# Flamingo block on one core: a new order of a layer unit, paired normalisations, resident inputs and two weight slots, with the bias accumulator in SBUF

## The reference

```python
for i in range(L):                                   # L = 4
    y = _attention(_norm(x), ctx, dist, mask, Wq[i], Wk[i], ...)   # 16 heads of 64
    x = x + y
    y = relu(_norm(x) @ Wf1[i] + bf1[i]) @ Wf2[i] + bf2[i]         # 512 wide
    x = x + y
# in _attention:
hbias   = relu(dist[..., None] @ Wth + bth)          # K = 32 terms for each pair of tokens
qs_bias = (hbias @ Wto + bto)[..., 0]
logits  = q k / 8 + mask + qs_bias                   # the same bias for all heads
```

## Time and profile before

| what | value |
|---|---|
| median of 3 runs | 1356.88 us (1356.79 to 1357.87) |
| profiled execution, its own time | 1357.18 us |
| span from the first to the last instruction | 1355.5 us |
| mean granted TensorE clock | 0.985 |
| first score, last F score group | 58.18 us, 1343.3 us |

### The profile page before, as it was taken

The page is one execution under the profiler, slowest core; times in us unless marked ns, Lnnn a source line. Parts: engine busy times, 40 slices in busy tenths (PEclk is TensorE's granted clock), DMA queues, the critical chain, the costliest instruction groups (busy, mean ns, idle before and its releaser), DMA issues.

```text
span 1355.5 us, 37243 instructions
## 1 busy us (share of the span) xinstructions
PE 1240.9 (92%) x11184; PEld 1020.6 (75%) x11184; DVE 1227.6 (91%) x4922; ACT 1061.2 (78%) x3353; POOL 854.1 (63%) x889
## 2 busy tenths in 40 slices
PE   1599999999999999999999999999999999799998
PEld 1377878787878787878787878788777878677776
DVE  4899999999999999999999999999999988488886
ACT  4588878887888888888888888788887866388886
POOL 3677777777777777777777777777777743111110
PEclk9799999999999999999999999999999999799999
DMA  5201010102110100022000000111101000000000
GB/s 148 75 5 30 14 32 14 32 13 79 46 33 13 29 17 24 22 70 55 24 22 24 22 20 24 59 47 29 31 13 44 13 14 11 5 21 21 23 16 9
DMA packets 69190, 42.21 MB, mean 31 GB/s; under 512 B 14840, under 2 KB 63872, under 8 KB 68992
## 3 DMA queue, kind: packets, MB, share of 16 engines
q1 hardware_dynamic: 68992, 39.84, 10.2%
HBM read 23.29 MB, written 1.05 MB: 18 GB/s over the span
## 4 chain that ended last, share of the span: by engine, by line
DVE 27%; PE 24%; ACT 22%; issue 20%; POOL 5%; DMA 1%; DVEq 1%; ACTq 0%; SPq 0%; POOLq 0%
ACT prob L802 13%; DVE bias_acc L951 7%; ACT relu_z L785 5%; PE L L688 4%; POOL sd L1391 4%; PE M L582 4%; PE O L552 4%; DVE score L998 3%; DVE hid L1073 3%; DVE qT L1123 3%; PE T L695 2%; DVE st L1016 2%; PE M L762 2%; DVE rs L1025 2%; ACT probT L809 1%
## 5 line engine op out<-in xcount | busy, mean ns | idle before, releaser
L802 ACT ACTIVATE prob<-score,nmax 128x128 f32<-128x128 f32 x1024 | 396.8, 391 | 156.5 <-DVE nmax L998 156.4
L1396 POOL TENSOR_TENSOR prob<-prob,rinv 128x512 f32<-128x512 f32 x256 | 291.6, 1139 | 178.4 <-DVE rinv L1006 173.2
L951 DVE SCALAR_TENSOR_TENSOR bias_acc<-relu_z,cst,bias_acc 128x512 f32<-128x512 f32 x370 | 349.8, 945 | 3.5 <-ACT relu_z L785 0.2
L785 ACT ACTIVATE relu_z<-dist_g,cst 128x512 f32<-128x512 f32 x386 | 295.1, 804 | 16.8 <-DMA cst<-cst_all 16.8
L998 DVE CUSTOM_DVE_ANT_0 score<-L,bias 128x128 f32<-128x128 f32 x1024 | 234.0, 281 | 2.7 <-PE L L528 1.6
L1391 POOL TENSOR_TENSOR sd<-mv,half 128x1 f32<-128x1 f32 x128 | 127.7, 998 | 118.3 <-DVE mv L1018 117.1
L802 ACT ACTIVATION_READ_ACCUMULATOR prob<-score,nmax 128x1 f32 x1024 | 193.6, 189 | 0.0
L538 PE MATMUL T<-ident,prob 128*128 128x128 f32 x1024 | 161.3, 280 | 4.8 <-POOL prob L1396 2.5
L582 PE MATMUL M<-wv,ctxT 128*128 128x512 f32 x256 | 145.6, 651 | 17.9 <-DVE hid L1073 13.0
L552 PEld LDWEIGHTS O<-probT,v 128*64 128x64 f32 x2048 | 109.7, 136 | 59.7 <-issue 51.9
L528 PE MATMUL L<-kT,qT 64*128 64x128 f32 x2048 | 149.7, 286 | 0.0
(11 more groups left out here) (134 smaller groups left out, 2225.8 us busy)
## 6 DMA issues: line engine op xcount, KB each, us to landing
dist_g<-in_fside_BxSxS SPq DMA_DIRECT2D x16, 256.0 KB, 2.9
mask_g<-in_mask_Bx1x1xS_ff SPq DMA_DIRECT2D x16, 256.0 KB, 3.5
ctxT<-ctxT_all SPq DMA_DIRECT2D x64, 64.0 KB, 1.9
xs<-x_all SPq DMA_DIRECT2D x64, 64.0 KB, 1.8
x_all<-xs SPq DMA_DIRECT2D x64, 64.0 KB, 1.8
wk<-in_L_xattn_Wk SPq DMA_DIRECT2D x4, 512.0 KB, 4.3
wv<-in_L_xattn_Wv SPq DMA_DIRECT2D x4, 512.0 KB, 5.4
wq<-in_L_xattn_Wq SPq DMA_DIRECT2D x4, 512.0 KB, 5.5
```

Source lines behind the costliest of these rows:

```text
L785: nc.scalar.activation(relu_z[:, z_slot(g, k), :], dist_g[:, :, :], ACT.Relu, bias=cst[:, C_BTH + k:C_BTH + k + 1], scale=cst[:, C_WTH + k ...
L802: last = nc.scalar.activation(prob[:, c, m, :], score[:, c, m, :], ACT.Exp, bias=nmax[:, c, m:m + 1], scale=-1.0, accum_out=rsum[:, c, m:m ...
L951: vec.scalar_tensor_tensor(out=bias_acc[:, :], in0=relu_z[:, z_slot(g, k), :], scalar=weight, in1=bias_acc[:, :], op0=ALU.mult, op1=ALU.ad ...
L1396: gp.tensor_tensor(prob[:, c, :, :], prob[:, c, :, :], rinv[:, c, :].rearrange("p (m o) -> p m o", o=1).broadcast_to([P, 4, P]), ALU.mult) ...
```

## The change

The units keep their work, and each engine has a new list. Bias terms: DVE takes 22 of a group and POOL 10; the accumulator `bias_acc` stays in SBUF. dist, mask, constants, x and context stay resident and are read in place, so the small copies by DMA go; the weights have two slots. The two normalisations of a step (the second of unit i-1 and the first of unit i+1) are done together: one root of two columns, one copy of both turned halves. `hid` is one instruction of 128x512; the hidden bias is folded into it and into the bias of the output. ACT makes all four copies of turned probabilities and both of the queries, DVE both of the keys and half of the output copies. The eight PSUM banks are shared out anew: the second score bank is the feed-forward bank (B0). In the F block the two groups of scores are written in turn, row group against row group.

```diff
-VEC_K = 24
-POOL_K = BIAS_K - VEC_K
+VEC_K = 22
+POOL_K = BIAS_K - VEC_K
+Z_PLAN = ((1, 1, 1, 3), (1, 1, 1, 3), (1, 1, 1, 2), (1, 1, 1, 2))
+TERM_PLAN = ((1, 1, 3, 1), (1, 1, 3, 1), (1, 1, 2, 1), (1, 1, 2, 1))
+POOL_PLAN = ((1, 2, 5), (1, 2, 5), (1, 2, 4), (1, 2, 4))
...
-cst = sb("cst", [P, C_ALL])
+dist_all = sb("dist_all", [P, BATCHES, P])
+mask_all = sb("mask_all", [P, BATCHES, P])
+wq = sb("wq", [P, 2, HEADS * HD])
+ACC = sb("bias_acc", [P, GROUP * P])
+hh = sb("hh", [P, 2, 2, P])
...
+S_BANK = [B[2], B[0], B[6], B[1]]
+T_BANK = [B[5], B[2], B[1], B[3]]
+K_BANK, V_BANK, Q_BANK, O_BANK = [B[2], B[3]], [B[4], B[1]], [B[6], B[4]], [B[4], B[5]]
+WO_BANK, HH_BANK, FF_BANK = B[3], B[6], B[0]
...
+    def scores(u, octet):
+        s = u % 2
+        if octet == 0:
+            pe.wait_ge(k_kept, upto(u, 2, 1))
+            pe.wait_ge(q_kept, upto(u, 2, 1))
+            wait(pe, pT_kept, upto(u - 1, 4, 1))
+            wait(pe, hid_kept, upto(u - 2))
...
-    def f_scores(g, i, c):
-        wait(pe, fexp, after(g, i, 4, c - 2))
-        rows = slice(32 * c, 32 * c + 32)
-        for j in range(ROW_HEADS):
-            last = mm(L[c % 2][:, j * P:(j + 1) * P], qm[rows, i % 2, j, :], kF[rows, i % 2, :], start=True, stop=True)
-        last.then_inc(fqk, 1)
+    def f_scores(g, i, half_):
...
+        wait(pe, fexp, after(g, i, 4, 2 * half_ - 1))
+        for j in range(ROW_HEADS):
+            for a in range(2):
+                c = 2 * half_ + a
+                rows = slice(32 * c, 32 * c + 32)
+                last = mm(L[a][:, j * P:(j + 1) * P], qm[rows, i % 2, j, :], kF[rows, i % 2, :], start=True, stop=True)
...
+    def inverse_deviation(i):
+        s, h = (i + 1) % 2, halves(i)
...
+    def normalise(u, a):
...
+        vec.tensor_scalar(hh[:, s, a, :], x_all[:, b, :], mv[:, s, a, 0:1], rs[:, s, a:a + 1],
+                          ALU.subtract, ALU.mult).then_inc(hb_done if a else ha_done, 1)
+    def keep_pair(i):
+        s, h = (i + 1) % 2, halves(i)
+        dve.wait_ge(hh_done, pairs(i))
...
+        vec.tensor_copy(hhT[:, s, h, :], src).then_inc(hh_kept, 1)
...
-                last = vec.tensor_scalar(hid[:, i % 2, c, :], M1[:, c * P:(c + 1) * P], bf1c[:, c:c + 1], 0.0, ALU.add, ALU.max)
+    def hidden(u):
...
+        vec.tensor_tensor(hid[:, u % 2, :, :], FF_BANK[:, :].rearrange("p (c t) -> p c t", c=CHUNKS),
+                          nb1_all[:, l, :].rearrange("p (c o) -> p c o", o=1).broadcast_to([P, CHUNKS, P]),
+                          ALU.max).then_inc(hid_kept, 1)
...
-        gp.tensor_tensor(sd[:, a, s:s + 1], mv[:, a, s, 1:2], half[:, 0:1], ALU.pow).then_inc(sdev[a], 1)
+    def root(i):
...
+        gp.tensor_tensor(sd[:, s, h], mv[:, s, h, 1], half[:, 0:h.stop - h.start], ALU.pow).then_inc(rooted, 1)
...
+    def step(i):
+        cur, prev = there(i), there(i - 1)
+        plan = POOL_PLAN[i % GROUP]
+        if cur:
+            norm(i, 0)
+            ops(plan[0])
+            norm(i, 1)
...
+            f_root(0, F_EARLY.index(i), 0)
+        if cur:
+            norm(i, 2)
+            ops(plan[1])
+        if prev:
+            plus_bias(i - 1)
+        if cur:
+            norm(i, 3)
```

More of the change, by code:

```diff
@@ L38 @@
 BIG = 3.0e38
-VEC_K = 24
+VEC_K = 22
 POOL_K = BIAS_K - VEC_K
 START_VEC_K = 26
-START_POOL_SKIP = START_VEC_K - VEC_K
-POOL_FIRST = 2
+START_POOL_K = BIAS_K - START_VEC_K
 Z_SLOTS = 6
[L49 to L83, removed]
+Z_LEAD = 3
+POOL_LEAD = 6
+Z_PLAN = ((1, 1, 1, 3), (1, 1, 1, 3), (1, 1, 1, 2), (1, 1, 1, 2))
+TERM_PLAN = ((1, 1, 3, 1), (1, 1, 3, 1), (1, 1, 2, 1), (1, 1, 2, 1))
+POOL_PLAN = ((1, 2, 5), (1, 2, 5), (1, 2, 4), (1, 2, 4))
+assert sum(map(sum, Z_PLAN)) == sum(map(sum, TERM_PLAN)) == VEC_K
+assert sum(map(sum, POOL_PLAN)) == 3 * POOL_K
+START_Z = (6, 4, 4, 3)
+START_STATS = (4, 4, 6)
+F_EARLY = (UNITS - 3, UNITS - 2)
+F_FIRST_PARTS = ((0, 1), (2, 3, 4, 5, 6), (7, 8, 9), (10, 11))
 C_WTH, C_BTH, C_WTO = 0, BIAS_K, 2 * BIAS_K
@@ L270, in block_program @@
         block = stack.enter_context(nc.Block())
[L272 to L294, removed]
@@ L498, in _ @@
+            for i in range(BATCHES):
+                sp.wait_ge(fout, i + 1)
+                sp.dma_start(out[i, :, :], outF[:, i % 2, :]).then_inc(out_st[i % 2], 16)
             for a in range(2):
@@ new lines, in ffn2 @@
+            def ffn2(u):
+                weights(u, w_f2)
+                pe.wait_ge(hid_kept, upto(u))
+                if there(u + 2):
+                    pe.wait_ge(scored, upto(u + 2, 4, 1))
+                for c in range(CHUNKS):
+                    last = mm(FF_BANK[:, 0:P], hid[:, u % 2, c, :], wf2[:, slot_of(u), c, :], start=c == 0, stop=c == CHUNKS - 1)
+                last.then_inc(f2_done, 1)
+            def step(i):
+                nxt, cur, prev, old = there(i + 1), there(i), there(i - 1), there(i - 2)
+                if cur:
+                    scores(i, 0)
+                    scores(i, 1)
@@ L1142, in f_first @@
+                if nxt:
+                    keep_keys(i + 1, 1)
+                more(2)
+                if prev:
+                    hidden(i - 1)
+                more(3)
+                if cur and i % GROUP == GROUP - 1 and i + 1 < UNITS:
+                    finish_bias(i // GROUP + 1)
             def f_first(g, i, part):
@@ L1372, in ahead @@
                     vec.tensor_scalar(bq_mask[:, :], head_mask[:, :], bqk[:, 0:1], None, ALU.mult).then_inc(f_consts, 1)
[L1374 removed]
+            f_step(0, -1)
+            step(UNITS)
+            f_step(0, 0)
+            residual2(UNITS - 1)
+            for i in range(1, BATCHES + 1):
+                f_step(0, i)
         @block.gpsimd
@@ new lines, in _, with ops, plus_bias @@
+            op_next = 0
+            def ops(n):
+                nonlocal op_next
+                for j in range(op_next, min(op_next + n, 3 * len(POOL_TERMS))):
+                    (product, clamp, add)[j % 3](j // 3, *POOL_TERMS[j // 3])
+                op_next += n
+            def plus_bias(u):
+                l = u // BATCHES
+                pool.wait_ge(resid1, upto(u))
+                wait(pool, resid2, upto(u - 2))
+                pool.wait_ge(bf_kept, l + 1)
+                gp.tensor_tensor(xb[:, u % 2, :], x_all[:, u % BATCHES, :], b2f[:, l % 2, :], ALU.add).then_inc(xb_done, 1)
```

1182 lines of the change are left out of this document (545 added, 637 removed).

## The result

The changed kernel takes 1369.78 us, median of four runs (1367.89 to 1371.05); the kernel before took 1356.84 beside it. The ratio is 1.0094 (95% interval 1.0077 to 1.0112): slower by 0.9%, where faster by 0.9% was forecast. The profiled execution takes 1371.05 us, its span is 1369.3 against 1355.5.

The account below looks back on a forecast made before the run. DVE, 95.5% busy, was taken to bound the layers, PE the F block. 1357.2 - 4 (start) + 1.5 (layers) - 9 (F block), less 0.3 for the median, gave 1345 us; range 1270 to 1390.

Parts of the forecast that it names:

- steady layers: Layer units: DVE's loop from `hid` to `hid`, 69.2 us a group against 69.1; +1.5 us over 15 groups.
- The F block: F units: scores in turn on two row groups save 0 to 1.27 us a unit; 0.6 taken, -9 us over 15 units.
- the start: Before the first scores: constants read in place let bias terms start up to 4.6 us earlier; -4 us taken.
- The waits between terms and POOL: Layers: a term waits for POOL's running instruction and ends 0.55 us after it; pairs take 1.68 or 1.18.
- the tosses: Layers: two near-ties between term and POOL, costing 0.63 and 0.76 us if lost; half counted, 68.5 to 69.2 a group.
- The price of `sde`: Layers: two-column `sde` may wait for POOL's second `norm`, up to 0.9 us a unit, +55; left outside the sum.
- the slower rival: Layers: POOL goes ahead at the second `h` in every step, +50 us less 10 already counted, 1385 us; chance 0.17.
- PE does not bind: Layers: PE's 16.4 us busy time a unit is partly waiting matmuls, its weight loads 13.7; PE sets no pace.

Follow-up runs that it names:

- the run with both edits: Changed kernel with `sde` as two single-column instructions and two extra PE matmuls in the wait ahead of every fourth unit's scores; 1314.42 us, ratio 0.9682.
- the filled wait: Changed kernel with two extra PE matmuls on resident data in the wait ahead of every fourth unit's scores; 1355.99 us, ratio 0.9985.
- the two runs on the width: Changed kernel with `sde` split into two single-column instructions, 1322.8 us; kernel before with that instruction alone widened to two columns, 1408.18 us.
- `hid` ahead of the terms: Changed kernel, accumulator in SBUF, with `hid` issued on DVE before the two or three terms of the third place; 1408.2 us, ratio 1.0358.

## Why the prediction was wrong

It was wrong in the sign, 25 us from forecast to result. The step that failed is the sum for the **steady layers**, which is 32 us off: it priced `sde` of two columns as one of one column (0.14, measured 1.00) and PE's wait for `hid` at nothing (measured 1.6 us wherever the clock fell). The F block gained 10 more than forecast and the start 3 less. Point by point:

- *The waits between terms and POOL*: right as a mechanism, a little long as a sum. The loop laid out by hand had 17.8, 17.7, 16.5 and 16.5 for the four kinds of step; with `sde` in single columns and the clock up they measure 17.36, 17.46, 16.43 and 16.28. The 0.55 behind a POOL instruction and the pairs of 1.7 and 1.2 stand in the trace, and with the accumulator in PSUM they are gone and 94 us with them, what the clock gave back included. With the tosses the text had 69.2 a group, 1.7 more than the 67.5 measured: in the step that it laid out in full POOL's next instruction goes ahead of the second `h`, which ends 10.7 us after `hid`, and with `sde` split that `hh` ends at 10.1 to 10.3 in three kinds of four. Over 15 groups the 1.7 are some 25 us the other way, so the errors partly cancelled and by luck the miss is smaller than its causes: without the two failed terms, in the run with both edits, the kernel takes 1314 us, 31 under the forecast.
- *The price of `sde`*: the first thing that failed. The text held it as a price that no row shows ("up to 0.9 a unit, +55"), put it outside the sum, and so took 0.14 of the one-column row for an instruction of two columns. It measures 1.00, and split it gives back 47 us, 41.6 of them without the clock. It costs 3.0 a group rather than four times 0.9, as the first `hh` would have waited for the same `norm` anyway; what it really moves is what comes behind it. That is also the mechanism of the slower rival, at its place: in steps of the first kind the `add` goes ahead of the second `hh`, and in those of the third the term falls behind the product.
- *PE does not bind*: the second thing. True of the loop, but the text priced PE's wait at nothing. A wait of 2.08 us ahead of the scores is followed by a low clock in most groups. Eleven steps of 18.6 rather than 16.9 us are 18.5 us, and the filled wait gave back 18.6. 67.5 + 3.0 is 70.5, with 1.6 in three groups of four 71.7. The 16.4 a unit by PE's busy time was indeed no floor: with the accumulator in PSUM and `sde` in two a unit takes 15.4, of which the weight loads are busy 13.5 (175.5/200 x 15.4).
- *The start*: terms do begin 3.65 us earlier (12.49 against 16.14), but the first score row is only 0.6 earlier. Twelve of the normalised inputs in one piece (6.09 us from 39.90) now stand ahead of the last twelve terms (10.29 from 46.44) and the first scores, where before four of the inputs stood in the same stretch. That is not all: the same list with the accumulator in PSUM has its inputs 3.4 us earlier, its twelve terms in 9.45, and the first score row at 53.45, 4.1 earlier. So the terms' waits for POOL cost about what the earlier start gave. No run tried the place of the inputs alone.
- *The F block*: the pitch came out as forecast (10.15 against the 10.1 of the text), 8.3 us over fifteen units, but by luck: the 0.6 was half of the bounds and not worked out. The text gave both groups of a unit's scores 2.14 us, where one of them takes 1.71. The run with the old order shows the two parts: the order is worth 0.98 a unit (11.13 less 10.15), and the rest of the new F block costs 0.42 (11.13 less 10.71). The other 10.5 of the gain are what the first two units took beyond the pitch: 19.1 and 13.86 before, 11.16 and 10.15 now. The text did not price them; that this comes from the new order of the last layer steps is argued from the trace, not tried. 11.16 itself is a lucky value: in six of the seven other runs of this kernel's variants that unit took 12.6 to 13.6.

The Trainium skill (VectorE: DVE Perf Modes, section What auto-detection actually checks) says that an instruction with a single source, in SBUF like its destination, runs in a mode that uses two ports when the outermost dimensions of both that are longer than one are even or equal, and (SBUF — State Buffer, section Who interferes with whom) that `copy`, `cast` and `tensor_scalar` can enter that mode and then contend with GpSimd. Two columns are an even count; the two runs on the width agree, 1.00 against 0.15, and so does the reciprocal, which is not in that list and takes 0.17. That a single column stays out of the mode is read from the runs. By that rule `sde` belonged into the sum.

## What to carry to other kernels

Two small instructions joined into one are not the same instruction: its shape can decide whether it waits for another engine, so price it by a row of the new shape or by a rule on shapes, and put the unknown price into the sum when what it meets is always there. A wait on an engine that is not the bound can still cost: look at the granted clock behind the longest wait of every period, and count what runs at the lower level. And when a loop through three engines sets the pace, taking away one engine's wait can gain nothing, as with `hid` ahead of the terms; ask which engine has no gap left.

## What had not been expected of the hardware

A `TENSOR_SCALAR` of 128x2 between SBUF tiles takes 1.00 us beside a 128x512 `norm` on GpSimd and 0.15 with 128x1, while a `RECIPROCAL` of 128x2 takes 0.17 beside the same instruction.

In the change a wait of 2.08 us on TensorE was followed by slow scores in eleven cases of fourteen (granted clock 0.63 over the stretch shown), waits of 1.5 to 1.6 us in none. The length of the wait alone does not decide: with `sde` in two it was five of fourteen after the same 2.08, and in the F block with the old order the clock fell in every second unit, behind waits of 0.98.

A root of two columns on GpSimd takes 0.70, against 0.55 for one where no term of VectorE stands ahead of it. In the layers of the kernel before, 119 of the 128 roots of one column met a term and took 0.97 to 1.10, ending 0.41 behind it: GpSimd waits for VectorE as well, even with an instruction of one column.

```profile
626.42 0.75 DVE L951 SCALAR_TENSOR_TENSOR bias_acc<-relu_z,cst,bias_acc 128x512 f32<-128x512 f32 x1
...
626.49 1.10 POOL L1391 TENSOR_TENSOR sd<-mv,half 128x1 f32<-128x1 f32 x1 [1.64 <-DVE mv L1018]
```
